# Count-matrix builder of a four-layer graph network: item dimension of the one-hots moved last, stores of cells issued by GpSimd

## What is computed

```python
x = layernorm(x + gin(x))          # two rounds of (x + segment_sum(x[src], dst)) @ W + b
x = layernorm(x + segment_sum(x[src] + x[dst] + edge_attr, dst))
x = layernorm(x + edge_mlp(x))     # two-layer MLP per edge, segment_sum by src, node MLP
x = layernorm(x + filter(x))       # degree-normalised products, segment_sum by src, leaky_relu
```

## Time and profile before

| what | value |
|---|---|
| median of three runs | 10942.0 us |
| time of the profiled execution | 10955.16 us |
| its span, first to last instruction | 10953.4 us |
| PE, DVE, ACT, POOL busy | 6082.3, 5266.2, 2226.6, 3602.8 us |
| granted TensorE clock, mean | 0.856 |

### The profile page before, as it was taken

The page is one execution under the profiler, slowest core; times in us unless marked ns, Lnnn a source line. Parts: engine busy times, 40 slices in busy tenths (PEclk is TensorE's granted clock), DMA queues, the critical chain, the costliest instruction groups (busy, mean ns, idle before and its releaser), DMA issues. The chain is left out here.

```text
span 10953.4 us, 166923 instructions
## 1 busy us (share of the span) xinstructions
PE 6082.3 (56%) x43186; PEld 5047.6 (46%) x43187; DVE 5266.2 (48%) x9074; ACT 2226.6 (20%) x4530; POOL 3602.8 (33%) x3345
## 2 busy tenths in 40 slices
PE   0123333333331556665147766777778778877696
PEld 0122333333331211111046766677777777777496
DVE  6666333333331799998133455233333333333344
ACT  0464000000000344444410000111111111111132
POOL 0001777777776000000000000344545545444100
PEclk9999999999999756665577888788898989898697
DMA  0200222222221222222154755222222222222263
GB/s 21 100 0 9 40 41 41 40 40 40 41 41 26 42 52 52 52 52 52 51 213 159 280 219 213 79 75 73 77 75 75 76 74 76 75 75 74 39 221 119
DMA packets 1450866, 876.35 MB, mean 80 GB/s; under 512 B 905023, under 2 KB 1376596, under 8 KB 1425535
## 3 DMA queue, kind: packets, MB, share of 16 engines
q1 hardware_dynamic: 1237570, 639.77, 20.4%
q0 software_dynamic: 106048, 137.48, 6.0%
q10 hardware_dynamic: 107136, 97.57, 2.5%
HBM read 713.06 MB, written 159.27 MB: 80 GB/s over the span
## 5 line engine op out<-in xcount | busy, mean ns | idle before, releaser
L653 POOL DMA_INDIRECT out_records<-scatter_recs,scatter_rows x1650 | 1958.9, 1187 | 1194.7 <-issue 1194.1
L1567 POOL DMA_INDIRECT edge_mlp_b_rows<-b_table,edge_mlp_recs x1664 | 1633.5, 982 | 2130.7 <-DMA edge_mlp_recs<-out_records 1626.1
L712 PE MATMUL scatter_sum<-scatter_attr,scatter_hot 128*128 128x65 f32 x3328 | 810.5, 422 | 1503.3 <-DMA scatter_attr<-in_edge_attr 1258.2
L712 PEld LDWEIGHTS scatter_sum<-scatter_attr,scatter_hot 128*128 128x128 f32 x3328 | 741.2, 328 | 1572.7 <-DMA scatter_attr<-in_edge_attr 1131.6
L1027 PE MATMUL pairs_p_ring<-pairs_hot_near,pairs_hot_far 128*128 128x512 f16 x2256 | 956.5, 575 | 726.2 <-ACT pairs_p_ring L1046 635.1
L1010 DVE TENSOR_TENSOR pairs_hot_near<-c_iota_wide,pairs_shift 128x4096 f16<-128x4096 f16 x282 | 1244.8, 4414 | 0.0
L1682 DVE CAST edge_mlp_hot_t<-edge_mlp_p_hot 128x512 f32<-128x512 bf16 x416 | 287.6, 691 | 1844.7 <-PE edge_mlp_p_hot L1611 1307.9
L1027 PEld LDWEIGHTS pairs_p_ring<-pairs_hot_near,pairs_hot_far 128*128 128x128 bf16 x2256 | 276.3, 122 | 1406.0 <-issue 1370.7
L760 DVE TENSOR_TENSOR nodes_wide_sums<-nodes_wide_sums,scatter_sum 128x65 f32 x1664 | 384.8, 231 | 1008.2 <-issue 857.2
L1621 PE MATMUL edge_mlp_p_pre<-edge_mlp_hot_t,edge_mlp_a_blk 128*128 128x128 f32 x3328 | 726.5, 303 | 197.8 <-DVE edge_mlp_hot_t L1682 145.6
L1104 POOL MEMSET sum_x_parts<- 128x192 bf16 x2 | 0.5, 260 | 2444.1 <-POOLq L123 2444.1
(11 more groups left out here) (419 smaller groups left out, 9559.0 us busy)
## 6 DMA issues: line engine op xcount, KB each, us to landing
sum_x_tiles<-edge_counts SPq DMA_DIRECT2D x78, 1536.0 KB, 7.6
edge_mlp_a_blk<-a_table SPq DMA_DIRECT2D x1664, 64.0 KB
edge_counts<-pairs_cells ACTq DMA_DIRECT2D x744, 128.0 KB, 1.7
sum_z_tiles<-edge_counts SPq DMA_DIRECT2D x48, 1920.0 KB, 7.8
sum_y_tiles<-edge_counts SPq DMA_DIRECT2D x39, 1536.0 KB, 7.7
scatter_attr<-in_edge_attr SPq DMA_DIRECT2D x1664, 32.0 KB
sum_x_tiles<-edge_counts SPq DMA_DIRECT2D x26, 1664.0 KB, 9.9
pairs_ends<-out_records SPq DMA_DIRECT2D x2256, 1.0 KB, 1.6
```

Of the source, the lines that this page charges most:

```text
L653: pool.indirect_dma_start(out=out_rec, out_offset=bass.IndirectOffsetOnAxis(ap=rows[s][:, c:c + 1], axis=0), in_=recs[s][:, c], in_offset= ...
L712: mm = pe.matmul(psum[s][:, c, 0:F + 1], hot[s][:, c], attr[s][:, c], start=True, stop=True)
L1567: pool.indirect_dma_start(out=b_rows[s][:, c], out_offset=None, in_=b_tab, in_offset=bass.IndirectOffsetOnAxis(ap=recs[s][:, c, FE + 1:FE ...
```

## The change

The item dimension of the one-hots and of the ramps goes last, so for one item the columns are 8 elements (16 bytes) apart, while each comparison has three operands whose last dimension is 8 consecutive 16-bit elements. The item's low end is first copied to bf16 by an instruction of its own, and `hot_far` now waits for `shift` and for this copy. The stores move from ScalarE's loop to one on GpSimd. Both load the numbers of four slots at a time.

```diff
-            nc.gpsimd.iota(k["iota_b"][:], [[1, P]], ...)
+            nc.gpsimd.iota(k["iota_b"][:], [[1, P], [0, BATCH]], ...)
-            nc.gpsimd.iota(k["iota_wide"][:], [[1, SUPER]], ...)
+            nc.gpsimd.iota(k["iota_wide"][:], [[1, SUPER], [0, BATCH]], ...)
...
-        hot_far = [sb(f"hot_far{s}", [P, BATCH, P], BF16) for s in range(BATCHES)]
-        hot_near = [sb(f"hot_near{s}", [P, BATCH, SUPER], FP16) for s in range(BATCHES)]
+        low = [sb(f"low{s}", [P, BATCH], BF16) for s in range(BATCHES)]
+        hot_far = [sb(f"hot_far{s}", [P, P, BATCH], BF16) for s in range(BATCHES)]
+        hot_near = [sb(f"hot_near{s}", [P, SUPER, BATCH], FP16) for s in range(BATCHES)]
...
-        stored = [st.sem(f"stored{s}") for s in range(RING)]
+        stored = k["dma_pairs"]
...
+        def slots_row(engine, name, it, s, low, top, why):
+            _, values = nc.values_load_multi_w_load_instructions(
+                rows[name][0:1, ds(it * RING + s, HALF)], engines=[engine], min_val=low, max_val=top,
+                skip_runtime_bounds_check_because=why)
+            return values
...
+        @block.gpsimd
+        def _(pool):
+            pool.wait_ge(loaded, 16 * tables)
+            for it in steps(pool, rounds):
+                for s in range(RING):
+                    if s % HALF == 0:
+                        plane = slots_row(POOL, "plane", it, s, 0, PLANES - 1, "a plane of the table")
+                        cell = slots_row(POOL, "cell", it, s, 0, NB - 1, "a block of the plane")
+                    pool.wait_ge(copied, it * RING + (s + 1))
+                    pool.dma_start(planes[:, ds(plane[s % HALF], 1), ds(cell[s % HALF], 1)],
+                                   cells[s][:].unsqueeze(1).unsqueeze(1)).then_inc(stored[s], 16)
+            for s in range(RING):
+                pool.wait_ge(stored[s], rounds * 16)
...
-                    low = ends[s][:].bitcast(BF16)[:, :, 1]
-                    dve.tensor_tensor(hot_far[s][:], bc(k["iota_b"][:], 1, BATCH), bc(low, 2, P),
+                    dve.tensor_copy(low[s][:], ends[s][:, :, 0]).then_inc(shifted[s], 1)
+                    dve.wait_ge(shifted[s], it * 2 + 2)
+                    dve.tensor_tensor(hot_far[s][:], k["iota_b"][:], bc(low[s][:], 1, P),
                                       ALU.is_equal).then_inc(hots_made[s], 1)
-                    dve.wait_ge(shifted[s], it + 1)
-                    dve.tensor_tensor(hot_near[s][:], bc(k["iota_wide"][:], 1, BATCH), bc(shift[s][:], 2, SUPER),
+                    dve.tensor_tensor(hot_near[s][:], k["iota_wide"][:], bc(shift[s][:], 1, SUPER),
                                       ALU.is_equal).then_inc(hots_made[s], 1)
...
-                            pe.matmul(p_ring[:, ds(banks[c], 1), :], hot_far[s][:, c], hot_near[s][:, c], ...)
+                            pe.matmul(p_ring[:, ds(banks[c], 1), :], hot_far[s][:, :, c], hot_near[s][:, :, c], ...)
...
-                    at = ds(it * RING + s, 1)
-                    until = nc.values_load(rows["until"][0:1, at], engines=[ACTIVATION], ...)
-                    plane = nc.values_load(rows["plane"][0:1, at], engines=[ACTIVATION], ...)
-                    cell = nc.values_load(rows["cell"][0:1, at], engines=[ACTIVATION], ...)
-                    act.wait_ge(done, until)
+                    if s % HALF == 0:
+                        until = slots_row(ACTIVATION, "until", it, s, 1, ITEMS, "how many items end the slot")
+                    act.wait_ge(done, until[s % HALF])
                     wait_count(act, stored[s], it * 16)
                     act.copy(cells[s][:], p_ring[:, s]).then_inc(copied, 1)
                     act.wait_ge(copied, it * RING + (s + 1))
                     act.mul(p_ring[:, s], p_ring[:, s], 0.0).then_inc(evicted, 1)
-                    act.dma_start(planes[:, ds(plane, 1), ds(cell, 1)], cells[s][:].unsqueeze(1).unsqueeze(1)).then_inc(stored[s], 16)
-            for s in range(RING):
-                act.wait_ge(stored[s], rounds * 16)
```

More of the change, by code:

```diff
@@ L57 @@
 BATCHES = 3
+HALF = 4
 CELL_SLOTS = -(-(CELLS + EXTRAS) // RING) * RING
@@ L169, in _ @@
                            allow_small_or_imprecise_dtypes=True)
-            nc.gpsimd.iota(k["iota_b"][:], [[1, P]], base=0, channel_multiplier=0,
+            nc.gpsimd.iota(k["iota_b"][:], [[1, P], [0, BATCH]], base=0, channel_multiplier=0,
                            allow_small_or_imprecise_dtypes=True)
-            nc.gpsimd.iota(k["iota_wide"][:], [[1, SUPER]], base=0, channel_multiplier=0,
+            nc.gpsimd.iota(k["iota_wide"][:], [[1, SUPER], [0, BATCH]], base=0, channel_multiplier=0,
                            allow_small_or_imprecise_dtypes=True)
@@ L719, in alloc_constants @@
     k = {n: ctx.enter_context(nc.sbuf_tensor("c_" + n, s, F32)) for n, s in shapes.items()}
-    k["iota_b"] = ctx.enter_context(nc.sbuf_tensor("c_iota_b", [P, P], BF16))
-    k["iota_wide"] = ctx.enter_context(nc.sbuf_tensor("c_iota_wide", [P, SUPER], FP16))
+    k["iota_b"] = ctx.enter_context(nc.sbuf_tensor("c_iota_b", [P, P, BATCH], BF16))
+    k["iota_wide"] = ctx.enter_context(nc.sbuf_tensor("c_iota_wide", [P, SUPER, BATCH], FP16))
     for n, w in (("blk_out", CHUNKS), ("unsorted", 1), ("extra_far", P), ("extra_near", P)):
@@ L1026, in _ @@
                         for c in range(4 * half, 4 * half + 4):
-                            pe.matmul(p_ring[:, ds(banks[c], 1), :], hot_far[s][:, c], hot_near[s][:, c], start=False, stop=True,
+                            pe.matmul(p_ring[:, ds(banks[c], 1), :], hot_far[s][:, :, c], hot_near[s][:, :, c], start=False, stop=True,
                                       skip_group_check=True).then_inc(done, 1)
@@ L1860, in gnn_stack @@
             k["dma_" + name] = [ctx.enter_context(nc.semaphore(f"dma_{name}{s}")) for s in range(SLOTS)]
+        k["dma_pairs"] = [ctx.enter_context(nc.semaphore(f"dma_pairs{s}")) for s in range(RING)]
         constants(nc, k)
```

## The result

The changed kernel takes 11188.26 us (median of four runs, 11175.91 to 11217.37), the kernel before 10932.96 us (four runs). The ratio is 1.0235, with a 95% interval of 1.021 to 1.0261. I forecast 10620 us. The profiled execution of the kernel after took 11175.91 us, its span is 11174.3 us.

What follows compares the result with a forecast made beforehand. VectorE and ScalarE bound the builder; SyncE's load issues would next, at 5.0 us a batch: 3637 + 1410 + 8 + tail 167 = 5222 instead of 5558, ramps +4, so -332 from 10955.2: 10620 us; range 10550 to 11180.

Steps and rivals of the forecast that it cites:

- SyncE's part: Builder's small loads, one issue per item: 5.0 us a batch, 1410 us in all, with VectorE and TensorE below it.
- Rival one: Builder's matmuls: strided operands make TensorE the bound, 865 ns a matmul, +203 us, 11158 us; chance 0.39.
- 330 bytes are not 16: Argument that line 563's matmuls, with 330 bytes between columns, may not price columns 16 bytes apart.
- If the column cost goes with the clock: Builder's matmuls: a strided one would take 0.43 us at 2.4 GHz, which fits below 5.0 us a batch.
- the row at 330 bytes: Line 563: 165 matmuls of 49 columns at 94 ns each, taken as a strided 16-bit column costing twice, 1.67 ns.
- The plain share of the same row: Line 563's 94 / 49 per column, giving 975 ns a builder matmul and +450 us.
- ScalarE and the stores: Builder's slots: ScalarE falls from 2.52 to 1.3 us each; GpSimd's stores take 1.55 us, tail 167 us instead of 280.
- VectorE: Builder's two comparisons: 4.41 to 2.28 us and 1.21 to 0.68 us, so 3.4 us a batch.
- Rivals two and three: Comparisons stay at 1.04 ns an element, 10849 us, chance 0.05; GpSimd's stores are the bound, 10906 us, chance 0.04.
- SyncE as the next bound: Builder after the change: SyncE's load issues set the pace at 5.0 us a batch.
- The ramps: Start of the kernel: wide ramp grows from 512 to 4096 columns, +3.5 us, narrow one +0.7, together +4 us.

Runs made afterwards that it cites:

- the five matmuls in 1.76 us: Kernel after with four matmuls of 512 consecutive columns against zero weights put ahead of each strided one: 12061.84 us.
- the stores alone: Kernel before with only stores on GpSimd and numbers loaded by fours, one-hots unchanged: 10654.55 us against 10892.97 for the kernel before.
- the version with two items: Kernel after with two items in the last dimension, columns and weights 4 bytes apart: ratio 0.9677 to the kernel before.

## Why the prediction was wrong

**The step that failed** is the line in SyncE's part: "TensorE at 8 matmuls of 0.427 us = 3.4 us ... both fit below 5.0". It took the pace of consecutive columns for columns 16 bytes apart. The measured 8 x 0.906 = 7.25 us does not fit: TensorE, not SyncE, set the pace of the builder, and the 1410 us from the first issue to the last became 2043 us from the first matmul to the last.

**The rival had the mechanism.** Rival one gave 865 ns and 11158 us; the runs show 906 ns and a median of 11188 us. I held it to be less likely than the forecast (0.39) on two grounds, and both fell. "330 bytes are not 16": 16 and 32 bytes cost nearly the same, 906 and 920 ns, so the row at 330 bytes was the right neighbour: at the 1.80 ns a column of 32 bytes its 49 columns are 88 of its 94 ns. "If the column cost goes with the clock": it does not, as the five matmuls in 1.76 us show; and the clock did not rise either, though TensorE never paused. The earlier trace rows showed a rise within the first 6.8 us of consecutive columns, and I carried it over to columns of another kind.

That the rival's price came so near is in part luck. It took the double of the half-clock pace, 2 x 0.83 = 1.67 ns a column, because a strided 16-bit matmul was as long as a float32 one. The runs show a cost that has nothing to do with that pace or with the clock: 1.77 ns for a new 16 bytes. The plain share of the same row, 94 / 49 = 1.92 ns, lay on the other side of it.

**The range** missed by 8 us at its upper end, because it ended 22 us above the rival's point value of 11158. The mis-sized terms of the rival's sum: 41 ns more for a matmul are +92 us; the tail at 1.14 us a slot in place of 1.55 is -44; the step from the last store to the next pass, +9, was not in it. With the 36 us that the rest took less this gives 11179, 3 us from the profiled execution. The prediction had the 975 ns of the plain share as the upper bound of that cost and left it out of the range.

**Slips in the working.** 512 x 94 / 49 is 982 ns, not 975. The forecast's own lower end does not follow from its terms: 0.3 us less in 282 batches and 0.35 us less in 108 slots are 122 us, so it should be 10500 and not 10550. And the sum starts SyncE at 3637 us, where its first issue stands at 3627.1. None of the three changes the outcome.

**ScalarE and the stores: right.** ScalarE takes 1.12 us a slot in the tail for the 1.3 taken, and the stores alone give -238 us. GpSimd's issue was bounded from indirect DMAs at 0.94 us and over and is 0.54 us; ScalarE, not GpSimd, paces the tail.

**VectorE: right.** 2.28 and 0.68 us forecast, 2.285 and 0.693 measured. Rivals two and three did not occur.

**SyncE as the next bound: right once TensorE is out of the way.** 5.0 us a batch was forecast; the version with two items has 5.10 us, and halving the loads takes it to 3.16, sharing them to 3.7.

**The ramps** were put at +4 us and take 8.5 us more on GpSimd. How much of it reached the path is not shown: the starts of the first matmul scatter by 10 us.

## What to carry to other kernels

A layout serves two readers: what makes the writer fast (the last dimension in consecutive 16-bit elements) can make the reader slow, and both have to be priced with the distance in bytes between the elements that each takes in turn. Here groups of two items gave VectorE its full gain and cost TensorE almost nothing; eight cost it the double of its pace at half clock, and four times its pace at full clock. Where the trace has one row with the same kind of access, even far off in size, it should weigh more than a reason why it might not apply, and its bounds belong in the range.

## What the runs showed that I had not expected

A strided moving operand (the columns) costs TensorE 1.77 ns for each new 16 bytes, at either clock. Consecutive 16-bit columns need 0.42 ns each at 2.4 GHz, so the cost shows from 8 bytes apart at full clock (453 in place of 216 ns for 512 columns), but hardly at half clock (453 in place of 427).

TensorE stayed at 1.2 GHz for 2.9 ms without a pause when each strided matmul of 0.91 us had one consecutive one beside it, and went at 2.4 GHz with four. A busy share of 100% in the windows says nothing of the clock, and nor does a clock of 1.00 where no change is on record: there the spacing of a matmul with consecutive columns tells it.

A plain store of 128 KB is issued by GpSimd in 0.54 us, shorter than its indirect DMAs of 128 rows (0.94 and 1.19 us); it lands after 2.0 us in place of 1.7.
